# The first group's sine products in PSUM, one bank for each 128 rows, in a fused adaLN, attention and FFN kernel

## The chip, the cores and the metric

The kernel runs on one core of a Trainium2 chip. The metric is the device time of one execution in microseconds (us), lower is better; the number of a version is the median of several executions. TensorE does the matmuls and writes PSUM, VectorE and ScalarE work on SBUF and PSUM, GpSimd works on SBUF, and SyncE starts the transfers here. Each engine runs its own list of instructions in order, and they meet only at semaphores.

## The reference

The input x is 64 x 64 x 256 (4096 tokens of 256 features), computed in float32:

```python
def rotate(x, delta_t, amplitudes, frequencies):
    a = amplitudes[None, :] ** delta_t[:, None]
    ang = frequencies[None, :] * delta_t[:, None]
    c, s = a * cos(ang), a * sin(ang)
    xr = x.reshape(Bn, Fn, 2, -1)
    x0, x1 = xr[:, :, 0], xr[:, :, 1]
    out0 = c[..., None] * x0 - s[..., None] * x1
    out1 = s[..., None] * x0 + c[..., None] * x1
x1 = x + retention(rotate(x), W_qkv, W_o, log_gamma)   # q, k (layer-normed per head), v, decay per head
x  = x1 + ffn(pool(x1, W1, b1, v, prompt types))       # int8 fake-quantised gate, up and down matmuls
```

The rotation pairs the two halves of a token's 256 features as the kernel lays them out: left' = c * left - s * right, and right' = s * left + c * right, with one c and one s for each token row.

## The kernel before

The 4096 tokens are cut into eight groups of 512 (`G = 8`), and each group into four blocks of 128 rows (`PP = 4`). Stage one runs over the groups: rotate x, project it to keys, queries and values, form scores and decays, sum, project out, add the residual, and pool. Stage two is the quantised FFN over blocks of 1024 tokens. Every engine's list is written out by hand, in four functions under one block, and the waits on semaphores are explicit, so the order is that of the code.

Groups 1 to 7 are rotated by GpSimd in the transposed layout (`rotate`, L537). Group 0 goes another way, since nothing else can run before it. Its rows lie in `x1[1]` (SBUF, a piece of the large tile `arena`), 128 rows by 4 blocks by 256 features.

- VectorE forms the angles. ScalarE takes their sines (L648 to L651; those of group 0 and 1 go to columns 0 to 7 of PSUM banks 2 and 3). GpSimd forms the amplitudes by a power (L514). VectorE multiplies them to `cs` (L1400 and L1401) and signals `cs1_ok`.
- ScalarE forms eight products of a 128 x 128 piece of x with the sine of the row, L657: for the left half of the output the four blocks of the right half of x, then the other way round. They go to `rot`, in SBUF, with a place for each of the eight; each signals `rot_part`.
- VectorE combines, L1408: eight instructions SCALAR_TENSOR_TENSOR, x times cosine, minus or plus the product, to `xrot` in SBUF. The last one of the left half signals `rot_left`, the last one of the right half `rot_done`.
- TensorE, after clock-keeping matmuls on the identity (L1054, from L1102) and eight transposes of cosine and sine to banks 4 and 5 (L1106), waits for `rot_left`, transposes four blocks to bank 6 (L1111), waits for `rot_done`, and transposes four more to bank 7. Behind each four stands one clock-keeping matmul to bank 0.
- ScalarE copies the two banks to `xT` (L743) and cosine and sine to `cs_rows` (L746). VectorE meanwhile rounds the centred key weights (L1413), takes their low part (L1415) and that of x (L1418). TensorE multiplies for the keys (L1118, L1122, L1126) in banks 0 and 1, and then for the queries in banks 2 and 3.
- Behind that VectorE takes the low parts of the query and value weights (L1427), the arguments of the decays (L1436) and the cosine and sine products of groups 2 to 7 (L1441, L1442). It copies the sums of the squared keys (L1423) when TensorE has them (L1080), iterates for the inverse root (L1520 to L1530), and multiplies by the decays (L1464).

GpSimd's list at this time is: centre the key weights (L528), cast the query weights (L531) and the value weights (L533) from SBUF to SBUF, the power for the other groups (L514), five small instructions on the masks (L505 to L509, L585, L586), and then the rotation of group 1 (L546 to L554) and the low part of its copy (L560). Its rotation of a later group waits for SyncE's transfers of cosine and sine.

Of the kernel before, what the change touches and what calls it, by code (L numbers as in the profile page):

```python
# [7 lines left out]
ALU = mybir.AluOpType  # L8
ACT = mybir.ActivationFunctionType
# [7 lines left out]
P = 128  # L17
# [5 lines left out]
DC = D // P  # L23
HC = NH // DC
QR = HC // 2
HW = D // 2
PP = 4
# [32 lines left out]
def build(nc, x, x_t, row, kinds, cols, w_qkv_t, w_o_t, w_o, w1, w_gate, w_up, w_down, out):  # L60
# [7 lines left out]
    with ExitStack() as ctx:  # L68
# [7 lines left out]
        bank = [psum[:, 512 * i:512 * i + 512] for i in range(8)]  # L76
# [18 lines left out]
        xrot = xrot_flat.rearrange("p (n d) -> p n d", n=PP)  # L95
# [5 lines left out]
        rot_flat = carve(2 * TG)  # L101
        rot = rot_flat.rearrange("p (r n d) -> p r n d", r=2, n=PP)
        rotT = rot_flat.rearrange("p (r t) -> p r t", r=2)
# [529 lines left out]
        def _(act):  # L633
# [20 lines left out]
            for h in range(2):  # L654
                other = x1[1][:, :, HW:D] if h == 0 else x1[1][:, :, 0:HW]
                for n in range(PP):
                    act.activation(rot[:, h, n, :], other[:, n, :], ACT.Identity, scale=cs[:, 1, n:n + 1]).then_inc(rot_part, 1)  # L657

# [239 lines left out]
        def _(pe):  # L898
# [153 lines left out]
            def keep_clock(times, o, w, rows):  # L1052
                for _ in range(times):
                    pe.matmul(o, w, rows, start=True, stop=True)  # L1054
# [46 lines left out]

            keep_clock(14, bank[0][:, 0:P], ident[:, :], ident[:, :])  # L1102
            pe.wait_ge(cs1_ok, 1)
# [3 lines left out]
            last.then_inc(csr_tr, 1)  # L1107
            for k, half in enumerate((rot_left, rot_done)):
                pe.wait_ge(half, 1)
                for p in range(PP):  # L1110
                    last = pe.transpose(bank[6 + k][:, p * P:p * P + P], xrot[:, p, k * P:k * P + P], ident[:, :])  # L1111
                last.then_inc(xT_tr, 1)
                keep_clock(1, bank[0][:, 0:P], ident[:, :], ident[:, :])
            pe.wait_ge(wk_ok, 1)
# [239 lines left out]
        def _(dve):  # L1354
# [48 lines left out]
            dve.wait_ge(x0_in, 16)  # L1403
            for h, (sign, half) in enumerate(((ALU.subtract, rot_left), (ALU.add, rot_done))):
                cols = slice(HW * h, HW * h + HW)
                for n in range(PP):
                    dve.wait_ge(rot_part, PP * h + n + 1)
                    last = dve.scalar_tensor_tensor(xrot[:, n, cols], x1[1][:, n, cols], cs[:, 0, n:n + 1], rot[:, h, n, :], ALU.mult, sign)  # L1408
                last.then_inc(half, 1)

# [416 lines left out]
```

## Time and profile before

| what | us |
|---|---|
| median of 3 runs | 267.98 |
| range of these runs | 267.8 to 268.16 |
| the profiled execution, device time | 268.05 |
| its span, first to last instruction | 266.3 |
| TensorE busy | 253.2 (95%) |
| VectorE busy | 221.5 (83%) |
| ScalarE busy | 183.6 (69%) |
| GpSimd busy | 145.7 (55%) |

The profile was taken in one execution, which is 0.07 us above the median of the runs. Its times count from the first instruction of the span; 1.75 us of the device time lie outside the span. TensorE's granted clock is at the full level in each of the 40 slices of the page. Busy shares are averages over a start-up of some 20 us, the loop over groups and the FFN, so for a change in the start-up the instructions there are what is to be read.

### The profile page before, as it was taken

What the parts mean: (1) busy time and instruction counts of PE and PEld (TensorE: products, weight loads), DVE (VectorE), ACT (ScalarE), POOL (GpSimd) and SP (SyncE); (2) the same over time, 40 slices, a digit from 0 to 9 for tenths busy, and PEclk for the clock granted to TensorE, in tenths of its full rate; (3) what the DMA queues carried; (4) which work ended last, traced back from release to release, by engine and by line L of the source; (5) the groups of instructions that cost most, each with busy time, mean ns of one, the idle gap of its engine ahead of it and who ended that gap; (6) DMA issues with size and microseconds to landing.
All of it is one profiled execution on the core that took longest, in us unless ns stands there. A gap on an engine that the chain in (4) does not pass through costs nothing.

```text
span 266.3 us, 8458 instructions
## 1 busy us (share of the span) xinstructions
PE 253.2 (95%) x3524; PEld 175.3 (66%) x3529; DVE 221.5 (83%) x483; ACT 183.6 (69%) x327; POOL 145.7 (55%) x144
## 2 busy tenths in 40 slices
PE   5899999999999999999999999999889999998994
PEld 5778789588779778778868967956534434443331
DVE  4889678799789798858868877969879999999994
ACT  5795463473487679579578269067699899829990
POOL 6898595872880792395377151014034779740670
PEclk9999999999999999999999999999999999999999
DMA  5991406306303500940770250220049588000267
GB/s 166 326 307 35 138 2 218 103 0 201 120 2 98 222 2 4 289 90 2 238 142 2 81 140 2 81 81 4 0 113 167 129 218 326 0 0 0 105 249 280
DMA packets 30311, 31.20 MB, mean 117 GB/s; under 512 B 12929, under 2 KB 20673, under 8 KB 30273
## 3 DMA queue, kind: packets, MB, share of 16 engines
q1 hardware_dynamic: 30272, 30.66, 38.7%
q8 instruction: 28, 0.46, 0.7%
q14 instruction: 11, 0.08, 0.1%
HBM read 19.48 MB, written 8.42 MB: 105 GB/s over the span
## 4 chain that ended last, share of the span: by engine, by line
PE 73%; DVE 10%; ACT 9%; issue 4%; DMA 1%; POOL 1%; DVEq 0%; ACTq 0%
PE psum L904 17%; PE psum L1292 6%; PE psum L928 6%; PE psum L943 6%; PE psum L1065 4%; PE psum L1311 4%; PE psum L1010 3%; PE psum L1071 3%; PE psum L1067 2%; PE psum L1066 2%; PE psum L1072 2%; ACT silu L867 2%; PE psum L1069 2%; PE psum L985 2%; ACT silu L849 2%
## 5 line engine op out<-in xcount | busy, mean ns | idle before, releaser
L1464 DVE TENSOR_TENSOR arena<-psum,xq_mem 128x512 f32<-128x512 f32 x64 | 39.7, 683 | 5.7 <-PE psum L928 5.7
L560 POOL TENSOR_TENSOR xT_lo<-arena,xT 128x512 fp32r<-128x512 f32 x14 | 17.6, 1277 | 39.8 <-ACT xT L692 39.8
L1292 PE MATMUL psum<-xq_mem,guT 128*128 128x512 bf16 x151 | 33.8, 379 | 0.3
L1292 PEld LDWEIGHTS psum<-xq_mem,guT 128*128 128x128 bf16 x152 | 14.4, 98 | 19.4 <-DVE arena L1680 1.8
L1691 DVE TENSOR_REDUCE h_max<-arena 128x1 f32<-128x1024 f32 (+1 forms) x24 | 25.9, 1122 | 0.2
L849 ACT ACTIVATE silu<-psum,gu_x 128x1024 f32<-128x1024 f32 (+1 forms) x24 | 24.4, 1025 | 2.1 <-PE psum L1292 1.1
L692 ACT ACTIVATE xT<-arena 128x512 fp32r<-128x512 f32 x14 | 8.1, 622 | 25.1 <-PE psum L904 23.0
L674 ACT ACTIVATE arena<-psum,pmask 128x512 f32<-128x512 f32 x32 | 20.2, 686 | 0.3 <-PE psum L1072 0.2
L1311 PE MATMUL psum<-arena,dT 128*128 128x512 bf16 x78 | 18.8, 380 | 1.3 <-DVE arena L1750 0.6
L943 PE MATMUL psum<-arena 64*32 64x128 f32 x1024 | 19.4, 274 | 0.5 <-DVE arena L1464 0.5
L928 PE MATMUL psum<-arena 32*64 32x128 f32 x1024 | 19.7, 278 | 0.0
L943 PEld LDWEIGHTS psum<-arena 64*32 64x32 f32 x1024 | 13.8, 105 | 5.9 <-issue 5.9
L904 PE MATMUL psum<-wT,xT 128*128 128x256 f32 x64 | 17.5, 295 | 0.0
L928 PEld LDWEIGHTS psum<-arena 32*64 32x64 f32 x1024 | 15.6, 130 | 2.9 <-issue 1.5
L619 POOL CAST arena<-silu 128x1024 bf16<-128x1024 int8 (+1 forms) x9 | 9.6, 1095 | 14.3 <-DVE silu L1745 13.1
L904 PE MATMUL psum<-woT,yT 128*128 128x256 f32 x64 | 17.0, 287 | 0.0
L575 POOL TENSOR_TENSOR xq_mem<-kind,xq_mem 128x256 f32<-128x256 f32 x8 | 4.9, 613 | 21.6 <-DVE arena L1553 21.6
L904 PE MATMUL psum<-wT_lo,xT 128*128 128x256 f32 x64 | 16.7, 283 | 0.0
L904 PE MATMUL psum<-woT_lo,yT 128*128 128x256 f32 x64 | 16.7, 283 | 0.0
L1479 DVE SCALAR_TENSOR_TENSOR psum<-psum,pmask,arena 128x256 f32<-128x256 f32 x28 | 12.4, 488 | 5.0 <-ACT arena L681 5.0
L1680 DVE TENSOR_TENSOR arena<-psum,silu 128x1024 f32<-128x1024 f32 (+1 forms) x13 | 14.7, 1136 | 1.8 <-ACT silu L849 1.8
L1311 PEld LDWEIGHTS psum<-arena,dT 128*128 128x128 bf16 x80 | 7.1, 98 | 12.8 <-DVE arena L1750 1.6
(249 smaller groups left out, 720.8 us busy)
## 6 DMA issues: line engine op xcount, KB each, us to landing
arena<-in_x SPq DMA_DIRECT2D x9, 512.0 KB, 3.8
x_dram<-arena SPq DMA_DIRECT2D x8, 512.0 KB, 3.3
pooled<-x_dram SPq DMA_DIRECT2D x8, 512.0 KB, 5.3
out<-pooled SPq DMA_DIRECT2D x15, 256.0 KB, 2.1
xin<-in_x_t SPq DMA_DIRECT2D x7, 512.0 KB, 4.7
cs_rows<-cs_dram SPq DMA_DIRECT2D x12, 256.0 KB, 5.1
pooled<-in_w_qkv_t SPq DMA_DIRECT2D x3, 256.0 KB, 4.8
pooled<-in_w_down SPq DMA_DIRECT2D x1, 704.0 KB, 8.0
```

What stands on the lines that cost most here:

```text
L560: pool.tensor_tensor(xT_lo[:, k, :], xrotT[:, k, :], xT[:, k, :].bitcast(F32), ALU.subtract).then_inc(xl_ok, 1)
L674: act.activation(qblk[:, c, odd, :], Q_BANK[c][:, :], ACT.Identity, scale=pmask[:, odd:odd + 1]).then_inc(q_ok, 1)
L849: act.activation(silu_tile(n, v)[:, a:], gate_bank(v)[:, a:], ACT.Silu, scale=gu_x[:, 0, v:v + 1]).then_inc(silu_ok, 1)
L904: return pe.matmul(o, w(k), x(k), start=start, stop=stop) if stationary_w else pe.matmul(o, x(k), w(k), start=start, stop=stop)
L928: mm = pe.matmul(bank[S_BANK[r]][S * b:S * b + S, p * P:p * P + P], kT[rows, c, t:t + S], qblk[rows, c, :, t:t + S], start=True, stop=True)
L943: last = pe.matmul(Y_BANK[half][b][32 * r:32 * r + 32, at_y:at_y + P], v_rows[rows, p, at_v:at_v + 32], dec[rows, c, r, p, :], start=True, ...
L1292: mm = pe.matmul(in_order(o[:, 512 * half:512 * half + 512], 2 * n + half), gT[i][:, v, c, :], xq_rows(2 * n + half, c), start=(c == 0), s ...
L1311: return pe.matmul(o, dT[:, c, v, :], hid_q[:, U * n + 2 * v + half, 0:512], start=first, stop=last)
L1464: dve.tensor_tensor(dec[:, c, r, :, :], bank[S_BANK[r]].rearrange("q (n k) -> q n k", n=PP), two_heads, ALU.mult).then_inc(dec_done, 1)
L1479: dve.scalar_tensor_tensor(o, y_psum(b, half, 1), pmask[:, 1:2], y_rows(b, half), ALU.mult, ALU.add).then_inc(y_ok, 1)
L1680: dve.tensor_tensor(hid_step(n, v)[:, a:], up_bank(v)[:, a:], silu_tile(n, v)[:, a:], ALU.mult).then_inc(h_ok, 1)
L1691: dve.tensor_reduce(h_max[:, n, v:v + 1], hid_step(n, v), AX.X, ALU.max, apply_absolute_value=True).then_inc(hm_done, 1)
```

## The change

ScalarE writes the eight products to PSUM: that of block n to the first 128 columns of bank n, for the left half first, and for the right half to the same place again. VectorE reads them there. Since a bank is now used twice, a product of the right half waits until VectorE has read the bank: each of the four combinations of the left half increments `rot_left`, and TensorE waits for the fourth increment. As bank 0 now holds data, the clock-keeping matmuls ahead of and between the transposes write to bank 7, and the one behind the transposes to bank 7 writes to bank 0. The tile `rot` is gone.

```diff
@@ ScalarE @@
             for h in range(2):
                 other = x1[1][:, :, HW:D] if h == 0 else x1[1][:, :, 0:HW]
                 for n in range(PP):
-                    act.activation(rot[:, h, n, :], other[:, n, :], ACT.Identity, scale=cs[:, 1, n:n + 1]).then_inc(rot_part, 1)
+                    if h:
+                        act.wait_ge(rot_left, n + 1)
+                    act.activation(bank[n][:, 0:HW], other[:, n, :], ACT.Identity, scale=cs[:, 1, n:n + 1]).then_inc(rot_part, 1)
@@ TensorE @@
-            keep_clock(14, bank[0][:, 0:P], ident[:, :], ident[:, :])
+            keep_clock(14, bank[7][:, 0:P], ident[:, :], ident[:, :])
...
-            for k, half in enumerate((rot_left, rot_done)):
-                pe.wait_ge(half, 1)
+            for k in range(DC):
+                if k == 0:
+                    pe.wait_ge(rot_left, PP)
+                else:
+                    pe.wait_ge(rot_done, 1)
                 for p in range(PP):
                     last = pe.transpose(bank[6 + k][:, p * P:p * P + P], xrot[:, p, k * P:k * P + P], ident[:, :])
                 last.then_inc(xT_tr, 1)
-                keep_clock(1, bank[0][:, 0:P], ident[:, :], ident[:, :])
+                keep_clock(1, bank[7 * (1 - k)][:, 0:P], ident[:, :], ident[:, :])
@@ VectorE @@
-            for h, (sign, half) in enumerate(((ALU.subtract, rot_left), (ALU.add, rot_done))):
+            for h, sign in enumerate((ALU.subtract, ALU.add)):
                 cols = slice(HW * h, HW * h + HW)
                 for n in range(PP):
                     dve.wait_ge(rot_part, PP * h + n + 1)
-                    last = dve.scalar_tensor_tensor(xrot[:, n, cols], x1[1][:, n, cols], cs[:, 0, n:n + 1], rot[:, h, n, :], ALU.mult, sign)
-                last.then_inc(half, 1)
+                    last = dve.scalar_tensor_tensor(xrot[:, n, cols], x1[1][:, n, cols], cs[:, 0, n:n + 1], bank[n][:, 0:HW], ALU.mult, sign)
+                    if h == 0:
+                        last.then_inc(rot_left, 1)
+            last.then_inc(rot_done, 1)
```

No instruction changes its place on its engine. Lines move by one on ScalarE and TensorE's first part, by four on TensorE's and VectorE's parts behind that, by six further on.

ScalarE's list at the place, from the last sines to the copies of the transposed x. Before:

```order
L650 ACTIVATE ang<-ang 128x24
L651 ACTIVATE ang<-ang 128x24
L657 ACTIVATE arena<-arena,cs 128x128 [waits cs1_ok,x0_in]
L657 ACTIVATE arena<-arena,cs 128x128 x7
L743 ACTIVATE xT<-psum 128x512 [waits xT_tr,head_masks,consts]
L743 ACTIVATE xT<-psum 128x512 [waits xT_tr]
```

and with the change:

```order
L649 ACTIVATE ang<-ang 128x24
L650 ACTIVATE ang<-ang 128x24
L658 ACTIVATE psum<-arena,cs 128x128 [waits cs1_ok,x0_in]
L658 ACTIVATE psum<-arena,cs 128x128 x3
L658 ACTIVATE psum<-arena,cs 128x128 [waits rot_left] x4
L744 ACTIVATE xT<-psum 128x512 [waits xT_tr,head_masks,consts]
```

The order is the same; the outputs are in PSUM, and the last four products each have a wait for VectorE.

## Rows read from the trace of the kernel before

**Rows 1.** The page: busy time of each engine, share of the span, instructions.

```profile
PE 253.2 (95%) x3524; PEld 175.3 (66%) x3529; DVE 221.5 (83%) x483; ACT 183.6 (69%) x327; POOL 145.7 (55%) x144
```

**Rows 2.** The chain that ended last, 7 to 23 us: start us, us, what.

```profile
8.13 0.41 ACT arena L657
...
8.68 2.90 DVE arena L1408 x8
...
11.62 0.66 PE psum L1111 x4
...
21.31 0.74 DVE arena L1464 x2
```

**Rows 3.** ScalarE's timeline, all eight and the last: start us, us, instruction, count.

```profile
8.13 2.44 ACT L657 ACTIVATE arena<-arena,cs 128x128 f32<-128x128 f32 x8 [0.18 <-DVE cs L1401]
...
10.19 0.39 ACT L657 ACTIVATE arena<-arena,cs 128x128 f32<-128x128 f32 x1
```

**Rows 4.** VectorE's timeline in narrow windows, the eight combinations.

```profile
8.68 0.35 DVE L1408 SCALAR_TENSOR_TENSOR arena<-arena,cs 128x128 f32<-128x128 f32 x1 [0.64 <-ACT arena L657]
...
8.95 0.69 DVE L1408 SCALAR_TENSOR_TENSOR arena<-arena,cs 128x128 f32<-128x128 f32 x1
...
9.56 0.69 DVE L1408 SCALAR_TENSOR_TENSOR arena<-arena,cs 128x128 f32<-128x128 f32 x1
...
10.18 1.39 DVE L1408 SCALAR_TENSOR_TENSOR arena<-arena,cs 128x128 f32<-128x128 f32 x5
```

**Rows 5.** GpSimd's timeline in the same stretch.

```profile
8.74 0.76 POOL L531 CAST wT<-pooled 128x512 fp32r<-128x512 f32 x1
9.44 0.67 POOL L533 CAST wT<-pooled 128x512 fp32r<-128x512 f32 x1
10.08 4.20 POOL L514 TENSOR_TENSOR a_pow<-cols_sb,dt_b 128x24 f32<-128x24 f32 x1
```

**Rows 6.** Differences L1484: two of SBUF operands with GpSimd's instruction; groups by form.

```profile
181.38 0.66 DVE L1484 TENSOR_TENSOR yT_lo<-arena,yT 128x256 fp32r<-128x256 f32 x1
...
181.97 0.41 DVE L1484 TENSOR_TENSOR yT_lo<-arena,yT 128x256 fp32r<-128x256 f32 x1
...
181.04 0.73 POOL L580 TENSOR_TENSOR xq_mem<-xq_mem 128x256 f32<-128x256 f32 x1
...
L1484 DVE TENSOR_TENSOR yT_lo<-psum,yT 128x256 fp32r<-128x256 f32 x28 | 11.3, 424 | 1.3 <-ACT yT L686 0.6
```

**Rows 7.** Timelines of ScalarE and VectorE at 57 us: a handover with one wait.

```profile
57.11 0.38 ACT L686 ACTIVATE yT<-psum 128x256 fp32r<-128x256 f32 x1 [0.26 <-DVE psum L1479]
...
57.53 0.43 DVE L1484 TENSOR_TENSOR yT_lo<-psum,yT 128x256 fp32r<-128x256 f32 x1
```

**Rows 8.** ScalarE's timeline: sines to PSUM and to SBUF.

```profile
7.53 0.16 ACT L649 ACTIVATE psum<-ang 128x8 f32<-128x8 f32 x1
7.63 0.21 ACT L650 ACTIVATE ang<-ang 128x24 f32<-128x24 f32 x1
7.74 0.20 ACT L651 ACTIVATE ang<-ang 128x24 f32<-128x24 f32 x1
```

**Rows 9.** VectorE's and GpSimd's timelines, 16 to 18 us.

```profile
16.77 0.29 DVE L1441 TENSOR_TENSOR cs<-a_pow,ang 128x24 f32<-128x24 f32 x1
16.99 0.17 DVE L1442 TENSOR_TENSOR cs<-a_pow,ang 128x24 f32<-128x24 f32 x1
17.54 0.29 DVE L1423 TENSOR_SCALAR sq_sums<-psum 128x128 f32<-128x128 f32 x1 [0.38 <-PE psum L1080]
...
16.26 0.77 POOL L586 TENSOR_TENSOR xq_mem<-xq_mem 128x64 f32<-128x64 f32 x1
16.98 1.32 POOL L546 TENSOR_TENSOR arena<-xin,cs_rows 128x512 f32<-128x512 f32 x1
```

**Rows 10.** Group 1: GpSimd's low part and TensorE's first use of it.

```profile
25.64 2.50 POOL L560 TENSOR_TENSOR xT_lo<-arena,xT 128x512 fp32r<-128x512 f32 x2 [0.74 <-ACT xT L692]
...
29.80 0.40 PE L1071 MATMUL psum<-xT_lo,wT 128*128 128x512 f32 x1
```

More of the change, by code:

```diff
@@ L101, in build @@
         rot_flat = carve(2 * TG)
-        rot = rot_flat.rearrange("p (r n d) -> p r n d", r=2, n=PP)
         rotT = rot_flat.rearrange("p (r t) -> p r t", r=2)
```

## The prediction

> **What bounds the kernel now.** I read the page first, then the chain of waits, then the timelines of single engines around the changed lines. The page shows TensorE busy for 95% of the span [rows 1], which says nothing yet about a change of 16 small instructions near the start: what counts is whether they lie on the chain that ended last, and at what pace they run there. The chain of waits [rows 2] answers the first question. It enters the rotation of group 0 with ScalarE's first product at 8.13 us, stays on VectorE's eight combinations from 8.68 to 11.58, goes on over TensorE's transposes at 11.62, and is at the decay products of group 0 at 21.31. Nothing in it comes from a transfer or from GpSimd. So whatever ends the eight combinations earlier should move all that follows.
>
> Who sets the pace in the rotation? ScalarE's eight products run without a gap [rows 3]: they begin at 8.13, the last at 10.19, so one every (10.19 - 8.13) / 7 = 0.29 us, and they are all done at 10.58 (10.19 + 0.39). VectorE ends 0.99 us after that. Its timeline [rows 4] shows why. The first combination takes 0.35, the second 0.69 and the third 0.69, and the last five together 1.39, which is one every 0.26 us at 0.34 each ((1.39 - 0.34) / 4). The two long ones end at 9.64 and 10.25. GpSimd's two casts of the query and value weights [rows 5] end at 9.50 and 10.11: both long combinations end 0.14 us behind a cast that was running when they were issued. When GpSimd is in its long power from 10.08 on, which reads only 24 columns, the combinations are short again. So VectorE stands behind GpSimd twice, 0.35 us each time, falls 0.70 us behind ScalarE, and catches up only (0.29 - 0.26) us per step. The same happens later between other instructions [rows 6]: at 181.38 a difference of two SBUF operands takes 0.66 us over a GpSimd product that ends at 181.77, and the same instruction at 181.97, with GpSimd idle, takes 0.41. The form of it that takes one operand from PSUM and the other from SBUF averages 424 ns over 28 instances, though GpSimd is busy for 55% of the span [rows 1]; two or three stalls of 0.25 us among them would show in that mean.
>
> **The change part by part.** (a) ScalarE writes the eight products to PSUM instead of SBUF, and VectorE reads them there. The combination then has one SBUF operand, x, and one PSUM operand, the form that does not stall in [rows 6]. I take both stalls away: -0.35 each, -0.70 us of VectorE's time. Not all of it is gained, since VectorE must now wait for ScalarE's pace of 0.29.
>
> (b) The end of the last combination, worked out: the last product ends at 10.58 if its pace stays [rows 3]. Its write goes to PSUM. Two sines that write 8 columns to PSUM and two that write 24 to SBUF stand side by side [rows 8]: starts are 0.10 and 0.11 us apart, and durations 0.16 and 0.21; with 16 columns less in the first pair that leaves 0.00 for the pace and about 0.03 for the end. I take -0.02, between 0 and -0.03. From ScalarE's end to VectorE's start, the first pair in this place needed 0.14 (8.13 + 0.41 to 8.68, behind several semaphores), while a later single wait of the same kind needed 0.04 (57.11 + 0.38 to 57.53) [rows 7]. The last combination waits for one semaphore, so I take 0.07, nearer to the second. Its own duration is 0.34 [rows 4], plus 0.01 for the PSUM operand (424 ns against the unstalled 0.41 of the two-SBUF form [rows 6]). The end: 10.58 - 0.02 + 0.07 + 0.35 = 10.98, against 10.18 + 1.39 = 11.57 now. That is **0.59 us**. With each bound taken one way it is 0.64 (10.58 - 0.03 + 0.04 + 0.34 = 10.93), the other way 0.49 (10.58 + 0.14 + 0.36 = 11.08, with 0.02 for the operand).
>
> (c) The new waits of ScalarE. Product n of the second half overwrites bank n, so it waits for combination n of the first half. The fifth product is due at 8.13 + 4 x 0.29 = 9.29, and the combination that it needs ended at 9.03 already in the run before. The eighth is due at 10.19; the fourth product ends at 8.13 + 3 x 0.29 + 0.39 = 9.39, its combination at about 9.39 + 0.07 + 0.35 = 9.81, 0.38 before that. Nothing is paid. Queued behind these waits on ScalarE are the copies of the transposed x; if the waits cost after all, they are late too. Even with the two stalls still there, combination four would end at 10.52, the eighth product would slip to 10.6 and end at 11.0, and the eighth combination, now at 11.23, would not be later.
>
> (d) The count on the left half's semaphore is now four increments instead of one, and TensorE waits for the fourth, the same instruction. It comes at about 9.81 instead of 10.52. The transposes of the left half then start when TensorE is through with those of cosine and sine, and are off the chain, because the right half ends last. The clock-keeping matmuls only change banks (7 for 0, and 0 in the last one): same number, same size, no cost. No DMA and no GpSimd instruction is touched.
>
> (e) Does the 0.59 reach the end? Behind the rotation the chain is made of instructions that wait for one another, so they shift as a block. What does not shift is GpSimd, busy with its power until 14.28 and with the rotation of group 1 after it. Its first result that TensorE needs is the low part of group 1, ready at 25.64 + 2.50 = 28.14, and asked for at 29.80 [rows 10]; with everything 0.59 earlier it is asked for at 29.21, so 1.07 us are left. From there on GpSimd follows ScalarE and TensorE. I carry the full 0.59: 268.05 - 0.59 = 267.46 against the profiled execution, which is 0.07 above the median of the runs shown, so **267.39** against 267.98.
>
> **A measurement of this kernel** can tell about 0.2% from no change, which is 0.54 us. The forecast lies just beyond that.
>
> **Rivals.** First, VectorE's PSUM read is dear. VectorE's own pace may grow by only 0.03 us per instruction before it, not ScalarE, sets the time. At twice that, 0.06 more, the last combination ends at 8.68 + 7 x 0.32 + 0.40 = 11.32, a gain of 0.25: 267.73. The 0.01 of [rows 6] speaks against it: 6%. The Trainium skill (Perfetto Trace Analysis, Optimizing Scalar/DVE Operations) gives about 60 ns of access overhead for VectorE on SBUF and 125 on PSUM; by that, an estimate, this rival would be the forecast. The measured instances differ by 0.01, so I go by them.
>
> Second, ScalarE is faster into PSUM. VectorE then sets the pace from the start: 8.68 + 7 x 0.26 + 0.35 = 10.85, less 0.03 for an earlier first product, a gain of 0.75: 267.23. The two spacings of [rows 8] speak against it, though they are of other instructions: 7%. The same section of that page has 93 ns for ScalarE on SBUF and 51 on PSUM, without saying for which side of the instruction; this rival is what it would give if it held for the output.
>
> Third, the gain is taken back by the same port in another place. VectorE's two products for cosine and sine of the other groups, at 16.77 and 16.99, both with two SBUF operands, would come at 16.18, in the middle of two short GpSimd subtractions, the second of which ends at 17.03 [rows 9]. If it holds them, the first ends at 17.17 (0.14 behind, as above), and the copy of the key sums, wanted at 16.95, starts at about 17.35 instead of 17.54 now: 0.19 of gain left, 267.79. The 0.38 us of idle time ahead of that copy [rows 9] absorbs less than this. 12%.
>
> Fourth, slower: the same two products fall behind GpSimd's first long product of group 1, which takes 1.32 us and now starts at 16.98 [rows 9]. If it started before 16.18, it would end at 17.49, the first cosine product at 17.63, and the copy of the sums would start at about 17.80: 0.26 later than now, 268.24. It needs GpSimd to arrive 0.8 us earlier than it does. Without the combinations in its way it gains on the two casts (0.76 and 0.67, both about 0.67 if undisturbed) only 0.09, and its later small instructions are themselves held by VectorE. 6%.
>
> Fifth, the stall stays, because x is still read from SBUF and the result still written there. Then nothing is gained, and by (c) nothing lost: 267.98. The 28 instances of [rows 6], which also read one operand from SBUF and write to it, speak against it: 9%.
>
> **Numbers.** The forecast keeps 60%. Of this case about 43 points lie beyond 0.54 us, since its bounds are 0.49 to 0.64 and a median of a few runs moves by about 0.1 (the runs shown span 0.36); 17 points lie within. Faster by over 0.2%: 43 + 7 = 50%. Within 0.2%: 17 + 6 + 12 + 9 = 44%. Slower: 6%. The range goes from 267.1 (the second rival less that scatter) to 267.85 (the third plus a little); the fourth and most of the fifth are left out.
>
> **What would show it.** Right: all eight combinations at 0.34 to 0.36 us, none of 0.69 beside the casts; ScalarE's products still 0.29 apart; the right half's transposes at about 11.02 instead of 11.62; the key sums' copy at about 16.95 and the first decay product at about 20.7 instead of 21.31. Wrong: a combination of 0.69 (fifth rival), combinations more than 0.29 apart though ScalarE is ahead (first), or a cosine product above 0.5 us at 16 to 17.5 (third and fourth).

## The result, and the profile after

| what | before | with the change |
|---|---|---|
| median | 267.98 (12 runs) | **267.38** (12 runs) |
| range of these runs | 267.8 to 268.16 | 267.31 to 267.52 |
| the profiled execution | 268.05 | 267.31 |
| its span | 266.3 | 265.6 |

The ratio of the times is 0.9978 (95% interval 0.9969 to 0.9987): the kernel is 0.60 us faster, against a forecast of 0.59.

The page of the changed kernel, busy time of each engine (before: [rows 1]):

```profile
PE 252.3 (95%) x3524; PEld 174.4 (66%) x3529; DVE 221.4 (83%) x483; ACT 183.7 (69%) x327; POOL 145.3 (55%) x144
```

The sums tell almost nothing: VectorE is busy 0.1 us less, though two stalls of 0.35 us are gone from it. The reason is one instruction at 27 us, the low part of the output weights, with both operands in SBUF. In the kernel before and in the changed one:

```profile
27.66 1.04 DVE L1427 TENSOR_TENSOR woT_lo<-pooled,woT 128x512 fp32r<-128x512 f32 x1
```

```profile
26.98 1.77 DVE L1433 TENSOR_TENSOR woT_lo<-pooled,woT 128x512 fp32r<-128x512 f32 x1
```

GpSimd's two differences for group 1 end at 28.14 and at 28.20. The instruction used to begin 0.48 us before that end, and now begins 1.22 us before it, so 0.73 us of what the rotation lost as stalls is back here. It costs nothing: VectorE idles for 1.03 us further on, until 31.34, for an instruction of ScalarE, and that one begins 0.68 us earlier than before (30.75 instead of 31.43). The chain of waits says more at 7 to 23 us (start us, us, what), to be laid beside [rows 2]:

```profile
8.11 0.38 ACT psum L658
8.63 2.29 DVE arena L1412 x8
10.96 0.66 PE psum L1115 x4
...
11.84 1.20 PE psum L1122 x4
...
20.64 0.74 DVE arena L1470 x2
```

It goes the same way as before, with the eight combinations 0.6 us shorter, the right half's transposes at 10.96 instead of 11.62, and the decay product at 20.64 instead of 21.31. The combinations one by one are in the view of their source line (busy ns of the shortest, middle and longest; start of the first to start of the last):

```profile
L1412 DVE SCALAR_TENSOR_TENSOR arena<-arena,cs,psum x8: 343/346/350, 8.6 to 10.6; 128x128 f32<-128x128 f32 x8
```

No combination takes 0.69 us any more ([rows 4] had two). ScalarE's products, by the same view and by its timeline, and GpSimd's and VectorE's timelines:

```profile
L658 ACT ACTIVATE psum<-arena,cs x8: 351/352/371, 8.1 to 10.2; 128x128 f32<-128x128 f32 x8
```

```profile
8.11 2.41 ACT L658 ACTIVATE psum<-arena,cs 128x128 f32<-128x128 f32 x8 [0.18 <-DVE cs L1405]
```

```profile
9.23 0.61 POOL L530 CAST wT<-pooled 128x512 fp32r<-128x512 f32 x1 [0.45 <-DMA pooled<-in_w_qkv_t]
9.96 0.62 POOL L532 CAST wT<-pooled 128x512 fp32r<-128x512 f32 x1
```

```profile
8.63 2.27 DVE L1412 SCALAR_TENSOR_TENSOR arena<-arena,cs,psum 128x128 f32<-128x128 f32 x8 [0.62 <-ACT psum L658]
...
16.87 0.29 DVE L1429 TENSOR_SCALAR sq_sums<-psum 128x128 f32<-128x128 f32 x1 [0.61 <-PE psum L1081]
```

ScalarE's eight still run without a gap and begin (2.41 - 0.35) / 7 = 0.29 us apart, but one takes 0.35 us where it took 0.39 [rows 3]. In this one execution the transfers of the query and value weights landed late, so the casts came half a microsecond later than in [rows 5]; they still run beside combinations three to eight, and none of these is long. They also take 0.61 and 0.62 us, where the first took 0.76 before: the combinations had held the casts too. (In the other kernels below that leave the casts in their place, the first began between 8.69 and 8.83 in the profiled execution. Beside combinations with a PSUM operand they took 0.61 to 0.62 us there as well.)

### The profile page after: what moved, and what is told of

Its sections match the earlier page's. It is cut to its first block, busy times and chain, and to the rows that moved or that the text cites. A ratio compares the mean times of both kernels' runs of the same rounds, so it can differ in the third digit from the quotient of the medians.

```text
span 265.6 us, 8458 instructions
## 1 busy us (share of the span) xinstructions
PE 252.3 (95%) x3524; PEld 174.4 (66%) x3529; DVE 221.4 (83%) x483; ACT 183.7 (69%) x327; POOL 145.3 (55%) x144
## 4 chain that ended last, share of the span: by engine, by line
PE 69%; DVE 12%; ACT 11%; issue 5%; DMA 1%; POOL 1%; DVEq 0%; ACTq 0%
PE psum L905 17%; PE psum L929 6%; PE psum L944 6%; PE psum L1066 4%; PE psum L1315 4%; ACT silu L850 3%; PE psum L1011 3%; DVE arena L1686 3%; PE psum L1072 3%; PE psum L1068 2%; PE psum L1067 2%; PE psum L1073 2%; ACT silu L868 2%; PE psum L1296 2%; PE psum L1070 2%
```

## The experiments

The theory: VectorE stands behind GpSimd's casts when both of its operands lie in SBUF; with one in PSUM it doesn't, and that is the whole gain. The rivals: the gain comes from ScalarE's faster write to PSUM, or from the earlier, finer signals of the left half. The times are medians in us; each is beside runs of the kernel before on the same chip. The fourth column is the one execution that was profiled, from which the rows below come.

| kernel | median (runs) | before | profiled | ratio (95%) |
|---|---|---|---|---|
| left half's products in PSUM | 267.41 (11) | 267.97 | 267.31 | 0.9978 (0.9969 to 0.9986) |
| right half's products in PSUM | 267.98 (11) | 267.97 | 267.92 | 1.0001 (0.9992 to 1.001) |
| before, power ahead of the casts | 267.58 (11) | 267.97 | 267.79 | 0.9987 (0.9978 to 0.9996) |
| before, two casts more | 268.64 (10) | 267.98 | 268.63 | 1.0031 (1.0019 to 1.0042) |
| change, two casts more | 267.29 (8) | 267.98 | 267.20 | 0.9977 (0.9967 to 0.9987) |
| change, power ahead of the casts | 267.38 (10) | 267.98 | 267.38 | 0.9977 (0.9968 to 0.9986) |
| change, transposes by block | 267.04 (6) | 267.97 | 267.09 | 0.9965 (0.9953 to 0.9978) |
| change, first product by VectorE | 267.40 (11) | 267.93 | 267.19 | 0.9982 (0.9973 to 0.9991) |
| the last two together | 267.26 (8) | 267.93 | 267.36 | 0.9974 (0.9964 to 0.9985) |
| both, one more ScalarE instruction | 267.12 (5) | 267.93 | 267.12 | 0.9958 (0.9944 to 0.9972) |
| first product by VectorE, one more | 267.02 (5) | 267.93 | 267.18 | 0.9965 (0.9952 to 0.9977) |
| all three, fewer clock matmuls | **266.71** (5) | 267.98 | 266.75 | 0.9951 (0.9938 to 0.9965) |

### Half of the change at a time

The changed kernel with the right half's products back in SBUF:

```diff
+        rot = rot_flat.rearrange("p (r n d) -> p r n d", r=2, n=PP)
...
-                    if h:
-                        act.wait_ge(rot_left, n + 1)
-                    act.activation(bank[n][:, 0:HW], other[:, n, :], ...
+                    act.activation(rot[:, h, n, :] if h else bank[n][:, 0:HW], other[:, n, :], ...
@@ VectorE @@
-                    last = dve.scalar_tensor_tensor(..., bank[n][:, 0:HW], ALU.mult, sign)
+                    last = dve.scalar_tensor_tensor(..., rot[:, h, n, :] if h else bank[n][:, 0:HW], ALU.mult, sign)
```

> Only the four products of the left half go to PSUM, those of the right half to SBUF as before. Port theory (a combination with two SBUF operands waits for GpSimd's running cast, one with a PSUM operand does not): the left four take 0.34 to 0.35 us each. Of the right four one may meet the second cast: if that ends at 10.1, the rotation ends at about 11.0 and the gain is about 0.5 us (267.45 to 267.55); if the casts come some 0.5 us later because their weights land later, as in the profiled execution of the changed kernel (9.23 and 9.96), one of the right four takes about 0.6 and the end is near 11.2, a gain of 0.3 (267.7). Rival, the gain comes from ScalarE's and VectorE's handling of PSUM itself, spread over all eight: half of it, 0.3 us (267.7), with no combination over 0.4 us whatever GpSimd does.

And the other way round, the left half's products in SBUF and the right half's in PSUM, with `if h` turned about in both places:

> Only the four products of the right half go to PSUM. Port theory: with the casts at 8.74 and 9.44 both stalls fall on the left half and stay; the rotation ends where it did (11.57) and the time is 267.9 to 268.0. With the casts at 9.23 and 9.96 only one of the left four is held, to about 10.0, and the rest follows at 0.26 to 0.29 us, end near 11.2, 267.65. Rival (PSUM itself is faster): half of the gain, 267.7, and the same as the version with the left half in PSUM.

The left half alone gives the whole gain (267.41, just below what was expected), the right half alone nothing (267.98, as expected). The combinations by source line in the first of these:

```profile
L1411 DVE SCALAR_TENSOR_TENSOR arena<-arena,cs,psum x4: 343/343/349, 8.6 to 9.4; 128x128 f32<-128x128 f32 x4
...
L1411 DVE SCALAR_TENSOR_TENSOR arena<-arena,cs x4: 350/350/353, 9.7 to 10.6; 128x128 f32<-128x128 f32 x4
```

and in the second:

```profile
L1411 DVE SCALAR_TENSOR_TENSOR arena<-arena,cs x4: 340/522/696, 8.7 to 10.2; 128x128 f32<-128x128 f32 x4
...
L1411 DVE SCALAR_TENSOR_TENSOR arena<-arena,cs,psum x4: 335/335/336, 10.4 to 11.2; 128x128 f32<-128x128 f32 x4
```

What decides is which half meets the casts. In the first kernel they end at 9.86, just behind the start of the first two-SBUF combination at 9.69, which by the 0.14 us of [rows 4, 5] would be held until 10.00 and takes till 10.04 anyway. In the second the left half meets them, and two combinations have 0.69 us. The finer signals and the other banks are in both kernels, and ScalarE's waits in neither, so none of these makes the gain. ScalarE's faster write to PSUM is not settled by this pair, since in the second kernel VectorE is behind ScalarE anyway; the next experiment, in which no product goes to PSUM, settles it. Without a stall the two forms cost VectorE nearly the same: 0.335 to 0.35 us.

### The casts elsewhere, nothing in PSUM

The kernel before, with GpSimd's long power ahead of the two casts, so that it reads 24 columns instead of 512 beside the combinations:

```diff
+            powers(slice(2 * PP, NPAIR))
             pool.wait_ge(ld_q, 16)
             pool.tensor_copy(wT[:, 0, :, :], raw_qkv[:, :, 0:D]).then_inc(wqv_ok, 1)
             pool.wait_ge(ld_v, 16)
             pool.tensor_copy(wT[:, 2, :, :], raw_qkv[:, :, 2 * D:3 * D]).then_inc(wqv_ok, 1)
-            powers(slice(2 * PP, NPAIR))
...
             pool.wait_ge(pow_ok, 2)
+            pool.wait_ge(wqv_ok, 2)
             bounds(1)
```

> The kernel before, with its products in SBUF, but GpSimd does its power for the other groups (24 columns) ahead of its two casts instead of behind them, so that no cast runs beside the eight combinations. Port theory: no combination over 0.36 us, the rotation ends at 10.58 + 0.07 + 0.34, about 11.0, 0.57 us earlier than before, with nothing in PSUM; the time is 267.4 to 267.6, if the casts, which come at about 13.0 and 13.7 instead of 8.7 and 9.4, hold nothing else up (the low part of the query weights then starts at about 13.7; TensorE wants it near 14.8). Rival (the gain is PSUM's): 268.0, or worse by the later casts.

Its GpSimd and VectorE timelines:

```profile
8.75 4.31 POOL L514 TENSOR_TENSOR a_pow<-cols_sb,dt_b 128x24 f32<-128x24 f32 x1
13.00 0.61 POOL L532 CAST wT<-pooled 128x512 fp32r<-128x512 f32 x1
```

```profile
8.68 2.29 DVE L1409 SCALAR_TENSOR_TENSOR arena<-arena,cs 128x128 f32<-128x128 f32 x8 [0.64 <-ACT arena L658]
...
13.64 1.06 DVE L1428 TENSOR_TENSOR wT_lo<-pooled,wT 128x512 fp32r<-128x512 f32 x1 [0.42 <-POOL wT L532]
```

This is the cleanest of the runs. Both operands are in SBUF, the products are written to SBUF, and the rotation ends 0.60 us earlier all the same (10.97 against 11.57): the casts had been the cause, and PSUM is only one way around them. Of the 0.60 only 0.39 reaches the end between the medians. The casts are now late: the low part of the query weights waits 0.42 us for the first and then runs beside the second, 1.06 us against 0.68 in the changed kernel. That this costs the rest is argued from the trace and was not tested by itself: TensorE begins the query products 0.05 us behind the changed kernel (14.76 against 14.71) and is through with the first half of them 0.19 us behind it (16.35 against 16.16). The profiled execution is one of the two slow ones of the eleven (267.79; nine lie between 267.53 and 267.58); it loses 0.24 us more at about 140 us, and why is open.

The Trainium skill (SBUF — State Buffer, Who interferes with whom) says that a VectorE instruction with two SBUF inputs contends with a GpSimd instruction that reads SBUF, and that one with at most one SBUF input, outside the two-port modes, does not. The casts agree in both directions. The power reads SBUF too, and eight two-SBUF combinations beside it took 0.34 to 0.35 us each; what shows of the rule is on the power's side, 4.31 us here against 4.16 beside combinations with a PSUM operand. So in this case a GpSimd instruction that streams 512 columns in 0.6 us held VectorE for 0.35 us, and one that reads 24 columns in 4.3 us for at most 0.01.

### Two casts more

A dose: two further casts of the same size behind the value weights' cast, to a part of SBUF that nothing reads, once in the kernel before and once in the changed one.

```diff
             pool.tensor_copy(wT[:, 2, :, :], raw_qkv[:, :, 2 * D:3 * D]).then_inc(wqv_ok, 1)
+            pool.tensor_copy(<512 unused columns of arena>, raw_qkv[:, :, 0:D])
+            pool.tensor_copy(<512 more>, raw_qkv[:, :, 2 * D:3 * D])
```

> The kernel before, and GpSimd repeats its two casts of the query and value weights once more into unused SBUF, straight behind the two that are there, ahead of its power: four casts beside the combinations instead of two. Port theory: four combinations take 0.6 to 0.7 us instead of two, at the casts' pace, and the rotation ends at about 12.3 instead of 11.57: 268.6 to 268.8 (GpSimd itself is 1.3 us later, which its idle time ahead of group 1 should about hide). Rival: no change in the rotation, 268.0.

> The changed kernel with the same two extra casts. Port theory: all combinations stay at 0.34 to 0.36 us and the rotation ends at 10.9, as without the extra casts: 267.4, or up to 0.3 more (267.7) if GpSimd's low part of group 1 now comes too late for TensorE. If a PSUM operand only made the stall rarer, one or two combinations over 0.5 us would be seen, and 267.9 or more.

The combinations in the kernel before with four casts:

```profile
L1410 DVE SCALAR_TENSOR_TENSOR arena<-arena,cs x8: 337/522/699, 8.6 to 11.9; 128x128 f32<-128x128 f32 x8
```

and in the changed one with four casts:

```profile
L1414 DVE SCALAR_TENSOR_TENSOR arena<-arena,cs,psum x8: 340/346/348, 8.6 to 10.6; 128x128 f32<-128x128 f32 x8
```

With two operands in SBUF each cast holds one combination: the line has four near 0.69 us, the eight end at 12.25, and the kernel is 0.66 us slower. With one in PSUM four casts hold none, and the time does not rise. (The median was 0.09 us below the changed kernel's, but its eight times, 267.20 to 267.77, reach across all of that kernel's, so no difference is shown.)

### The power first, in the changed kernel

> The changed kernel with GpSimd's power ahead of its casts. Port theory: there is no stall left to remove, so the rotation ends at 10.9 as in the changed kernel and the time is 267.35 to 267.5. Rival, that a good part of GpSimd's interference is left in the changed kernel (combinations at 0.35 instead of 0.34, or later instructions of VectorE held by the casts): faster by 0.1 us or more, 267.25.

The edit is that of the power ahead of the casts. It came to 267.38, which is the changed kernel's time: the two cures do not add up, as they should not if they cure the same thing. The casts are late here too, but the cost is nearly absorbed. VectorE's timeline of this kernel:

```profile
17.24 0.28 DVE L1430 TENSOR_SCALAR sq_sums<-psum 128x128 f32<-128x128 f32 x1
...
20.05 0.23 DVE L1535 TENSOR_TENSOR psum<-psum,rs 128x64 f32<-128x64 f32 x1
```

The key sums' copy is 0.37 us later than in the changed kernel (16.87), the step of the inverse root only 0.09 (19.96 there). The rest is made up on TensorE, which takes the copied sums up only behind three more of its query products. Its first instruction that reads them, in the changed kernel and in this one:

```profile
17.54 0.27 PE L1088 MATMUL psum<-ident,sq_sums 128*128 128x128 f32 x1
```

```profile
17.59 0.31 PE L1089 MATMUL psum<-ident,sq_sums 128*128 128x128 f32 x1
```

In the changed kernel the copy ends at 17.16 and lies ready for 0.38 us; here it ends at 17.52, 0.07 before it is read. So that copy is not on the chain in either kernel. With both operands in SBUF the step stood at 20.20, 0.24 later.

### What bounds the rotation now: transposes by block

ScalarE's pace now sets the end of the combinations, and behind them come four transposes in a row on TensorE. They can start as the blocks come:

```diff
             for k in range(DC):
-                if k == 0:
-                    pe.wait_ge(rot_left, PP)
-                else:
-                    pe.wait_ge(rot_done, 1)
                 for p in range(PP):
+                    if k and p == PP - 1:
+                        pe.wait_ge(rot_done, 1)
+                    else:
+                        pe.wait_ge(rot_left, PP * k + p + 1)
...
-                    if h == 0:
+                    if h == 0 or n < PP - 1:
                         last.then_inc(rot_left, 1)
```

> The changed kernel, and TensorE waits for each combination by itself and turns its block at once, instead of waiting for four. The chain then has one transpose behind the last combination instead of four: 3 x 0.11 = 0.33 us less. ScalarE's copy of the right half starts at about 11.3 instead of 11.66. Theory that the rotation is on the chain and all behind it moves as a block: 267.05 to 267.15. Rival, that the next limit is near (VectorE's list of the rounded and low weights, or GpSimd's low part of group 1, asked for at 29.1 and ready at 28.2): nothing or under 0.1 us more, 267.3 to 267.4.

TensorE's and ScalarE's timelines of this kernel (the changed one: transposes 10.96 for 0.66 us):

```profile
10.34 1.07 PE L1115 MATMUL psum<-ident,arena 128*128 128x128 f32 x4
```

```profile
11.44 0.60 ACT L744 ACTIVATE xT<-psum 128x512 fp32r<-128x512 f32 x1 [0.28 <-PE psum L1115]
```

Three of the four transposes now lie beside combinations. The copy starts 11.44 - 8.23 = 3.21 us behind ScalarE's first product (at 8.23 in this execution), against 11.65 - 8.11 = 3.54 in the changed kernel; the 0.33 arrives at the end between the medians, 267.04. (Between the two profiled executions it is 0.22, since this one began its rotation 0.12 later.)

### The first product on VectorE, a result that was not expected

VectorE idles while ScalarE makes the first product. So let it make that product itself:

```diff
@@ ScalarE @@
+                    if h == 0 and n == 0:
+                        continue
@@ VectorE @@
+            link(dve.tensor_scalar(bank[0][:, 0:HW], x1[1][:, 0, HW:D], cs[:, 1, 0:1], None, ALU.mult))
...
-                    dve.wait_ge(rot_part, PP * h + n + 1)
+                    if h or n:
+                        dve.wait_ge(rot_part, PP * h + n)
```

> The changed kernel, and VectorE, idle from 8.03 to 8.63 us, forms the first of the eight products itself (x times sine into bank 0), so that ScalarE has seven. Theory that with the stalls gone ScalarE's pace of 0.29 us sets the end of the rotation: the last combination ends one pace earlier, near 10.62 instead of 10.91, and the time is 267.05 to 267.15. Rival, VectorE is already the pace (its combinations start every 0.26 to 0.29 us, and it now has one instruction more): the end moves by less than 0.1 us, 267.3 to 267.4.

Alone, and with the transposes by block:

> Both: TensorE turns each block as soon as it is combined, and VectorE forms the first product. If the two gains add (0.34 measured for the first, 0.29 expected for the second): 266.7 to 266.8, with TensorE's last transpose near 10.9. Rival, a limit comes in between them, VectorE's list of rounded and low weights (its two differences for the low part of x end near 13.2 now, and TensorE wants them at 13.4 in the version that turns by block) or GpSimd's low part of group 1: 266.9 to 267.0.

Both medians, 267.40 and 267.26, miss these forecasts. The rotation did its part. VectorE's timeline of the kernel with the first product alone:

```profile
8.07 0.35 DVE L1410 TENSOR_SCALAR psum<-arena,cs 128x128 f32<-128x128 f32 x1
8.46 2.18 DVE L1416 SCALAR_TENSOR_TENSOR arena<-arena,cs,psum 128x128 f32<-128x128 f32 x8
```

The eight end at 8.46 + 2.18 = 10.64 instead of 10.90, and TensorE stays ahead by as much until 43 us. There, in this execution, it is lost. TensorE's last value product of the group, and the copy on ScalarE that waits for it, in the changed kernel:

```profile
42.88 0.40 PE L905 MATMUL psum<-wT,xT_lo 128*128 128x256 f32 x2
...
43.38 0.64 ACT L693 ACTIVATE xT<-arena 128x512 fp32r<-128x512 f32 x1 [5.97 <-PE psum L905]
```

and with the first product on VectorE:

```profile
42.60 0.40 PE L907 MATMUL psum<-wT,xT_lo 128*128 128x256 f32 x2
...
43.40 0.63 ACT L695 ACTIVATE xT<-arena 128x512 fp32r<-128x512 f32 x1 [6.26 <-PE psum L907]
```

TensorE is done at 43.00 instead of 43.28, but ScalarE starts at 43.40 instead of 43.38: 0.40 us behind it instead of 0.10. The same 0.30 us more stood there in the kernel with both edits, and in no other kernel till then. Neither is the copy itself changed nor what it waits for. What is changed is its place: ScalarE's list has one instruction less ahead of it. So I put one back, of no use, in an idle stretch at 22 us. (The expectation below counts the distance from the semaphore event, so it says 0.04 and 0.34 to 0.36 us where the rows give 0.10 and 0.40.)

```diff
+        spare = sb("spare", [P, 1])
...
                 act.activation(v_rep[rows, h, :], ones[rows, 0:S], ACT.Identity, scale=v_col[rows, 0:1]).then_inc(v_rep_ok, 1)
+            act.activation(spare[:, :], f_col, ACT.Copy)
```

> The changed kernel with VectorE forming the first product, plus the same filler on ScalarE. Theory of the place in the list: 267.05 to 267.15, with 0.04 us ahead of the copy near 43 us. Rival: 267.35 to 267.45 as without the filler.

> The version with both, plus one ScalarE instruction that does nothing useful (a copy of one column into an unused tile, in ScalarE's idle time near 22 us). In the two versions in which VectorE forms the first product, ScalarE's list is one instruction shorter than in all others, and its copy of the transposed x of group 2, near 43 us, starts 0.34 to 0.36 us behind the event it waited for, against 0.04 in the nine others. Theory: the delay hangs on the place of that instruction in ScalarE's list (what the trace puts down to issue), so with the filler it is 0.04 again, the gain of the rotation is kept, and the time is 266.70 to 266.85. Rival, the delay hangs on the time at which the instruction is reached, or on the earlier rotation itself: it stays above 0.3 us and the time is 267.1 to 267.3.

The two timelines at the same place, first product on VectorE and one instruction more:

```profile
42.79 0.40 PE L909 MATMUL psum<-wT,xT_lo 128*128 128x256 f32 x2
...
43.28 0.63 ACT L696 ACTIVATE xT<-arena 128x512 fp32r<-128x512 f32 x1 [5.98 <-PE psum L909]
```

The distance is 43.28 - 43.19 = 0.09 again, as it is in the two other kernels with the filler. So the delay at this place hangs on how many instructions stand ahead on ScalarE, at least between these two counts. The median is 267.02, as expected, and all five times (266.97 to 267.18) lie below all eleven without the filler (267.19 to 267.82).

That the delay is the whole difference between the two medians is not shown. The profiled execution without the filler is the fastest of its eleven and the one with the filler the slowest of its five, and they end together, at 267.19 and 267.18. Without the filler the key sums' copy starts 0.26 us ahead of the changed kernel's (16.61 against 16.87), and the lead is gone only at 43 us. With the filler the lead is 0.09 there (16.78) and still 0.09 at 43 us: that execution lost the rest earlier, while TensorE was late with its start-up, as the next section tells. The spread of 0.63 us without the filler is not explained. The kernel with both edits lost more than the delay too: in its trace the lead over the changed kernel is 0.62 us at the key sums' copy, 0.38 at 25 us and 0.20 at 36 us, and after the delay it is 0.10 behind. The 0.42 lost before the delay lie on TensorE (its 64 small matmuls from 22.08 take 1.93 us against 1.64 in the best version, and one product at 32 us 0.38 against 0.24); no run shows why.

One thing in the traces goes with the delay. Queue 14, which the profile calls an instruction queue, moves 8 KB packets. In each of the twelve kernels without the delay one of them falls between 25 and 28 us. In the two kernels with it none falls between 22 and 46 us, and one falls between 46 and 47. The queue's row in the changed kernel at 25 to 27 us, and in the one with the first product on VectorE at 46 to 47.2 us (packets, MB, share of 16 engines):

```profile
q14 instruction: 1, 0.01, 1.7%
```

```profile
q14 instruction: 1, 0.01, 1.6%
```

So with the instruction that is missing in ScalarE's list this packet moves too. That the loading of instructions makes the delay would fit this, but it is not tested, and the packet comes 3 us behind the delay. What in the chip makes the delay is open.

### The start-up matmuls, and the best version

With all three edits the five times were 266.54, 266.70, 267.12, 267.14 and 267.14. They were expected between 266.70 and 266.85, so two are at the lower bound or below it, and three are 0.3 to 0.4 us above the range; the median, 267.12, is a miss. The profiled execution is one of the three (267.12). TensorE's and ScalarE's timelines:

```profile
3.33 6.15 PE L1059 MATMUL psum<-ident 128*128 128x128 f32 x28 [3.33 <-POOL ones L501]
9.32 1.04 PE L1111 MATMUL psum<-ident,cs 128*128 128x128 f32 x8
```

```profile
10.91 1.18 ACT L747 ACTIVATE xT<-psum 128x512 fp32r<-128x512 f32 x2 [0.69 <-PE psum L1119]
```

The 28 clock-keeping matmuls take 6.15 us here, 5.70 in the kernel before and 4.79 in the changed kernel's execution, and with them the transposes of cosine and sine end at 10.36, 9.91 and 9.16. Ahead of a rotation that ends at 11.6 or 10.9 this is hidden. Now it isn't: the left half's transposes queue behind it. ScalarE's row holds both of its copies, and the second, for the right half, starts at 10.91 + 1.18 - 0.60 = 11.49. (The profiled execution with the first product on VectorE and the filler, above, has the same: 6.24 us of these matmuls, and the transposes of cosine and sine end at 10.45.) So fewer of these matmuls are wanted:

```diff
-            keep_clock(14, bank[7][:, 0:P], ident[:, :], ident[:, :])
+            keep_clock(11, bank[7][:, 0:P], ident[:, :], ident[:, :])
```

> The version with both and the filler, and 11 clock-keeping matmuls at the start instead of 14 (22 records instead of 28). In the profiled execution of the version with 14, 26 of the 28 records took 0.42 us, 0.21 apart, and TensorE was through with the transposes of cosine and sine only at 10.36, behind six of the combinations; in other kernels' profiled executions 13 to 27 records were slow and that end lay between 9.16 and 10.45. Its times fell in two lots, 266.54 and 266.70, and 267.12 to 267.14. Theory: TensorE's arrival is the limit in the late executions; with 22 records, even all slow, it is through with them at 3.33 + 22 x 0.21 = 8.0 to 8.2, and with the transposes by 9.9, so all executions fall in the early lot: 266.55 to 266.75. Rival, the three matmuls were needed: with TensorE idle or slow before the transposes, these and the key products behind them stay at the slow pace, and the time is 267.1 or more.

TensorE's and ScalarE's timelines of this kernel, the latter with the right half's copy:

```profile
3.34 5.06 PE L1059 MATMUL psum<-ident 128*128 128x128 f32 x22 [3.34 <-POOL ones L501]
...
8.20 1.43 PE L1111 MATMUL psum<-ident,cs 128*128 128x128 f32 x8
```

```profile
11.06 0.60 ACT L747 ACTIVATE xT<-psum 128x512 fp32r<-128x512 f32 x1 [0.28 <-PE psum L1119]
```

TensorE is now through at 9.63, the right half's copy starts 0.43 us earlier, and the five times lie between 266.65 and 266.75. At the key sums' copy this execution is 0.55 us ahead of the changed kernel's, and it is 0.56 ahead at the end (266.75 against 267.31): nothing is lost on the way. That TensorE's arrival splits the times of the version with 14 is shown for its late lot only, since neither of its two early executions was profiled, and five times of each version are few. **266.71** is the best version found: 1.27 us below the kernel before, 0.67 below the changed one.

## Why the prediction was right

(a) *Both stalls go.* Right. The combinations took 0.343 to 0.350 us beside the casts, and the runs with half of the products in PSUM, with four casts and with the power first show that the casts were the cause and the PSUM operand the cure. This also closes rival five. The runs show whom the operand's place frees; by which path inside the chip, they do not show.

(b) *The end at 10.98.* It came at 8.63 + 2.27 = 10.90, 0.08 earlier. Three terms were a little off, all in the same direction. The write to PSUM took 0.035 us off a product's end (0.35 against 0.39), where I took 0.02. ScalarE started 0.02 earlier, of which 0.01 was left at its last product. And the last handover, estimated at 0.07 between 0.04 and 0.14, was just below its lower bound: the last product starts at 10.18 and takes 0.35, so it ends at 10.53, and the last combination starts at 10.56, 0.03 later. The combination's 0.35 was right. In the trace the gain is therefore 0.67 us (21.31 to 20.64), above my bound of 0.64. Between the medians it was 0.60, between the two profiled executions 0.74; the forecast of 0.59 met the median more closely than its terms deserved.

(c) *ScalarE's new waits cost nothing.* Right: its eight instructions stand in one row of the timeline with a pace of 0.29 us, and the kernel without the waits, with the right half back in SBUF, takes the same time (267.41).

(d) *Finer signals, transposes of the left half, other banks: nothing.* Right. The right half alone in PSUM has these too and gained nothing.

(e) *All of it reaches the end.* Right. The copy of the key sums moved from 17.54 to 16.87 and the decay product by 0.67. GpSimd's low part of group 1 and TensorE's first use of it:

```profile
25.69 2.51 POOL L559 TENSOR_TENSOR xT_lo<-arena,xT 128x512 fp32r<-128x512 f32 x2 [0.74 <-ACT xT L693]
```

```profile
29.12 0.39 PE L1072 MATMUL psum<-xT_lo,wT 128*128 128x512 f32 x1
```

It is ready at 28.20 and asked for at 29.12, so 0.92 us were left, against 1.07 in the forecast. The block moved by 0.67, but the copy of the key sums is not one of its links, as the run with the power first showed: TensorE takes it up 0.38 us after it is ready.

The rivals. The first, a dear PSUM read, is out: 0.335 to 0.350 us against 0.337 to 0.353 for the unstalled form from SBUF. By the Trainium skill's two figures for VectorE (Perfetto Trace Analysis, Optimizing Scalar/DVE Operations), about 60 ns on SBUF and 125 ns on PSUM, one operand in PSUM would have cost 0.065 us more, an estimate; the trace does not agree. The second, ScalarE faster into PSUM, is half true: the instruction is 0.035 us shorter, but the next one starts no sooner, and pace is what it needed. The Trainium skill's 93 and 51 ns for ScalarE (same page and section) differ by 0.042 us, an estimate of the gain that is near the 0.035 measured here, where only the output was moved. The third and fourth turned on VectorE's two products for cosine and sine of the other groups meeting GpSimd, first its two small subtractions, then its first long product. The two VectorE products and the long one in the changed kernel:

```profile
15.96 0.21 DVE L1447 TENSOR_TENSOR cs<-a_pow,ang 128x24 f32<-128x24 f32 x1
16.09 0.17 DVE L1448 TENSOR_TENSOR cs<-a_pow,ang 128x24 f32<-128x24 f32 x1
```

```profile
17.08 1.29 POOL L545 TENSOR_TENSOR arena<-xin,cs_rows 128x512 f32<-128x512 f32 x1
```

VectorE was through 0.8 us before the long product began, so the fourth did not happen. The third was not put to the test in this execution: with the casts late, the subtractions ran from 16.52 to 17.13, behind VectorE's products. They do meet in the kernel with transposes by block:

```profile
16.19 0.30 DVE L1447 TENSOR_TENSOR cs<-a_pow,ang 128x24 f32<-128x24 f32 x1
```

```profile
15.81 0.64 POOL L584 TENSOR_TENSOR xq_mem<-xq_mem 128x64 f32<-128x64 f32 x1
```

The product takes 0.30 us instead of 0.21, as it did in the kernel before (0.29 [rows 9]), and is not held until 0.14 behind the second subtraction (16.77). The third rival's price was wrong too: it took a delay of the key sums' copy as the same delay of the end. In the kernel with the change and the power first that copy started at 17.24, near the 17.35 of that rival, and the time was 267.38. What the same meeting did take back, 0.73 us of VectorE's time at 27 us, no rival had named; it was free. Of the fourth rival, the casts undisturbed take 0.61 us, not 0.67.

## What to carry to other kernels

When VectorE and GpSimd work side by side, look at the longest of several equal VectorE instructions, not at their mean: if the long ones all end at the same distance behind the end of a GpSimd copy (0.14 us here), they are waiting for it, and one of two SBUF operands moved to PSUM, or the GpSimd copy moved elsewhere, frees them. Only the pairs that meet need it (here moving four of the eight products was enough), and what is freed is worth only the distance to the next pace, 0.6 of 0.7 us here. When a change that should gain does not, compare the distance from releaser to start, instruction by instruction, and look for work that was hidden by what you have just removed.

## What was not expected of the hardware

- One ScalarE instruction at 43 us starts 0.40 us behind its releaser instead of 0.10 when one instruction less stands ahead of it in the list; one useless instruction at 22 us takes that back. The median goes from 267.40 to 267.02 with it, but the two profiled executions end together. An 8 KB packet of the instruction queue falls between 25 and 28 us in the kernels without the delay and at 46 us in those with it.
- The power on GpSimd, 4.2 to 4.3 us long, does not hold two-SBUF combinations, and is 0.15 us longer beside eight of them (4.31 against 4.16); a cast of 0.6 us does hold them, and is held in turn (0.76 and 0.67 against 0.61 and 0.62).
- The same 28 start-up matmuls took 4.79, 5.70 and 6.15 us in three executions, the changed kernel's, that of the kernel before and that of all three edits. What sets this is open. The granted clock reads full in all of them, as in this row of the last's windows (the stretch, its length, then busy us and instructions of PE, PEld, DVE, ACT and POOL, the granted clock, the share of the DMA engines and GB/s):

```profile
3.30:8.50 5.20, 5.17 (x24) 5.17 (x25) 4.24 (x22) 4.14 (x11) 3.57 (x7) 1.00 1.00 313
```
